# Experts begin on five full tiles of the first three batches, and the fourth batch is routed between their steps

## What is computed

```
# third layer, after the softmax and the weighting of the values
out = einsum('bnf,fd->bnd', out, Wout)
mu, var = mean(out), var(out)                       # over the 256 channels
out = (out - mu) * rsqrt(var + 1e-6) * ln_scale + ln_bias
x = x + tanh(g_xattn[1]) * out
# fourth layer, on X = layernorm(x)
logits = X @ Wg + bg                                # 8 experts
topv, topi = top_k(logits, 2); w = softmax(topv)
xs = X * w                                          # one row per token and choice
for e in range(8):                                  # H = 1024
    h = silu(xs @ W1[e]) * (xs @ W3[e]);  y = h @ W2[e]
    out = out + where(topi == e, y, 0).sum(choices)
x = x + tanh(g_ffn[1]) * (X + out)
```

## Time and profile before

| | us |
|---|---|
| median of 3 runs | 2034.28 (2030.84 to 2037.16) |
| the profiled execution | 2036.09 |
| its span, first to last instruction | 2034.4 |
| TensorE busy in the span | 1792.8 (88%) |
| VectorE busy | 1181.5 (58%) |
| ScalarE busy | 1116.2 (55%) |
| GpSimd busy | 423.8 (21%) |
| mean granted TensorE clock | 0.947 |

### The profile page before, as it was taken

How to read it: one execution, slowest core, us unless ns; L and a number is a source line. 1 busy time by engine, 2 the same in 40 slices (tenths; PEclk the granted TensorE clock), 3 DMA queues, 4 the chain that set the end, 5 groups by cost and what they waited for, 6 DMA issues and landing times. The chain is left out here.

```text
span 2034.4 us, 28113 instructions
## 1 busy us (share of the span) xinstructions
PE 1792.8 (88%) x9516; PEld 1121.3 (55%) x9516; DVE 1181.5 (58%) x2893; ACT 1116.2 (55%) x2334; POOL 423.8 (21%) x430
## 2 busy tenths in 40 slices
PE   5899998998996599999999999999982599999994
PEld 3455554554543234444444444445442599999994
DVE  4868768767772455545564465435644455555554
ACT  2566666666674155544554455445550467777662
POOL 3101200200201100000000002000202377766762
PEclk9999999999998699999999999899986799999997
DMA  3000000000000770000000001000001766666644
GB/s 94 1 21 1 21 1 1 22 1 1 1 1 0 263 245 1 21 1 0 1 21 1 0 1 43 1 0 1 23 1 51 249 212 202 203 208 214 217 152 140
DMA packets 122862, 134.13 MB, mean 66 GB/s; under 512 B 9248, under 2 KB 116640, under 8 KB 122720
## 3 DMA queue, kind: packets, MB, share of 16 engines
q1 hardware_dynamic: 115696, 119.45, 18.6%
q0 software_dynamic: 3744, 10.49, 1.4%
q10 hardware_dynamic: 3280, 2.40, 0.4%
HBM read 101.63 MB, written 30.69 MB: 65 GB/s over the span
## 5 line engine op out<-in xcount | busy, mean ns | idle before, releaser
L622 DVE TENSOR_REDUCE l_tile_max<-psum 128x1 f32<-128x512 f32 x512 | 341.8, 688 | 108.1 <-PE psum L345 106.7
L483 ACT ACTIVATE l_probs<-psum 128x1024 f32<-128x1024 f32 x256 | 248.3, 1022 | 99.3 <-PE psum L357 95.7
L345 PE MATMUL psum<-l_kT,l_qT 128*128 128x512 f32 x512 | 236.2, 469 | 40.9 <-DVE l_tile_max L622 37.6
L2013 POOL TENSOR_TENSOR moe_w_lo<-moe_w,moe_w_hi 128x512 fp32r<-128x512 f32 x179 | 233.2, 1303 | 139.6 <-ACT moe_w_hi L1886 138.9
L1380 DVE TENSOR_REDUCE l_row_max<-psum 128x2 f32<-128x1024 f32 x128 | 156.4, 1222 | 182.1 <-PE psum L1000 181.3
L1210 ACT ACTIVATE l_null_p<-l_s_null,l_neg_max 128x1 f32<-128x1 f32 x256 | 73.9, 289 | 285.2 <-DVE l_neg_max L1382 285.2
L1846 PE MATMUL psum<-moe_xs_hi,moe_w_hi 128*128 128x256 f32 x736 | 211.3, 287 | 1.4 <-DVE moe_xs_lo L1923 1.4
L1846 PE MATMUL psum<-moe_xs_lo,moe_w_hi 128*128 128x256 f32 x736 | 209.3, 284 | 0.0
L1846 PE MATMUL psum<-moe_xs_hi,moe_w_lo 128*128 128x256 f32 x736 | 209.3, 284 | 0.0
L1986 DVE TENSOR_TENSOR psum<-psum,moe_gate 128x256 f32<-128x256 f32 x184 | 79.3, 431 | 166.1 <-ACT moe_gate L1900 166.1
L1212 ACT ACTIVATE l_probs<-psum,l_neg_max 128x512 f32<-128x512 f32 x256 | 171.5, 670 | 0.0
(11 more groups left out here) (238 smaller groups left out, 3246.8 us busy)
## 6 DMA issues: line engine op xcount, KB each, us to landing
moe_w<-in_moe_w SPq DMA_DIRECT2D x276, 256.0 KB, 4.4
moe_sorted_x<-l_zeros SPq DMA_DIRECT2D x1, 17680.0 KB, 57.1
moe_xs<-moe_sorted_x SPq DMA_DIRECT2D x23, 272.0 KB, 2.9
l_ctxT<-in_ctxT SPq DMA_DIRECT2D x4, 1024.0 KB, 5.4
x_resid<-in_x SPq DMA_DIRECT2D x4, 512.0 KB, 10.1
l_raw<-in_ctx SPq DMA_DIRECT2D x4, 512.0 KB, 3.5
l_v_raw<-in_ctx SPq DMA_DIRECT2D x4, 512.0 KB, 3.6
l_wk<-in_wkv SPq DMA_DIRECT2D x1, 2048.0 KB, 16.1
```

The source lines that it names most:

```text
L345: nc.tensor.matmul(bank(max_bank(m)), qT[:, q % SLOTS, h, t * P:(t + 1) * P], kT[:, q % SLOTS, h // 2, half * BANK:(half + 1) * BANK], sta ...
L483: nc.scalar.activation(probs[:, n % PT_RING], wide(2 * (n % 2)), ACT.Exp, scale=SCALE).then_inc(exp_done, 1)
L622: nc.vector.reduce_max(tile_max[:, q % 2, t, h, half:half + 1], bank(max_bank(m)), AX_X).then_inc(max_read, 1)
L2013: nc.gpsimd.tensor_tensor(w13_lo[:, k % SPLITS], w13[:, slot_k, :, cols], w13_hi[:, k % SPLITS].bitcast(F32), ALU.subtract).then_inc(w13_s ...
```

## The change

- The router's buffers and steps move into a class `Router` that both layers use; what they compute is the same. In `layer1`, batch 2's routing is moved to earlier steps of `extra` (its norm now in groups 28 and 29, ranking in step (6, 0) in place of (6, 3), slots in (6, 2) in place of (7, 2)), and so are its PE and ACT parts. 
- The new number `FIRST` is 5: 3 batches of 512 tokens with 2 choices are 3072 rows, and with 8 experts at least 5 tiles of 256 rows are full whatever the routing. In the last group's idle DVE steps, `count_tiles`, `sum_tiles`, `note_used`, `list_experts` and `list_starts` list these five tiles.
- All of batch 3 that came after its projection leaves `layer1`. The block now ends with the projection.
- In `experts`, SP waits only for the scatter of three batches, loads tile 0's rows first, and then weights. For tile 5 it waits for the second list (`tiles_ready`), and loads that tile's rows after its weights, behind a wait for all scatters.
- Batch 3's work is cut into pieces that `route_last(k)` puts behind step k of each engine: PE at k = 10 (8 transposes), 12 (16 matmuls for the logits) and 17 (2 for the counts); ACT at 10, 17 (exponential) and 21 to 24 (scaling rows); DVE at 0 to 8, 10, 12, 14 to 18, 20, 22 to 26, 28, 29, 32 and 33; POOL at 22 to 29 (one scatter each).
- POOL splits w1 and w3 for the first five steps too. The `up` sums move to PSUM banks 4 to 6, both halves of a tile's result into one bank, and the copy out of it is one instruction.

```diff
+        self.FIRST = -(-(TOP * (self.T - self.TT) * P - self.E * (ROWS - 1)) // ROWS)
...
         else:
-            at = (first - 1, 1, 0), (first - 1, 1, 1), (first - 1, 2, 0), (first, 1, 0)
+            at = (first - 2, 2, 1), (first - 2, 3, 0), (first - 2, 3, 1), (first - 1, 1, 0)
...
-                keep_result(GROUPS - 1)
-                act.wait_ge(last_psum, 1)
-                nc.scalar.activation(rT[:, 0, :], bank(4), ACT.Copy).then_inc(last_act, 1)
-                weigh_second(s.B - 1)
-                for k in range(TOP):
-                    scale_rows(s.B - 1, k, range(T))
...
-                last_b = s.B - 1
-                dve.wait_ge(out_psum, T)
-                for _ in output_statistics(lambda t: bank(t)[:, 0:D]):
...
-                add_counts(last_b, bank(O_BANK))
-                choose_slots(last_b)
-                weigh_tops(last_b)
-                add_residual(last_b, range(T))
...
+        CHAIN = {"rT": 10, "logits": 12, "counts": 17, "exp": 17, "scale": 21, "scatter": 22}
...
-                sp.wait_ge(tiles_ready, 1)
+                sp.wait_ge(scattered, 16 * TOP * TB * LAST_B)
+                load_rows(0)
                 for m in range(PIECES):
-                    if m == W_SLOTS:
-                        sp.wait_ge(scattered, 16 * TOP * T)
-                        load_rows(0)
-                        load_rows(1)
                     i, part = divmod(m * PIECE, FT)
                     if part == 0:
+                        if i == FIRST:
+                            sp.wait_ge(tiles_ready, 1)
                         e = sp.value_load(expert_ids[0:1, i:i + 1], min_val=0, max_val=E - 1)
-                        if m >= W_SLOTS:
+                        if i >= 2 and i != FIRST:
                             load_rows(i)
                     load_weights(m)
+                    if m == 1:
+                        load_rows(1)
+                    if i == FIRST and part == FT - PIECE:
+                        sp.wait_ge(scattered, 16 * TOP * T)
+                        load_rows(FIRST)
...
+                round_weights(0)
+                round_rows(0)
+                for k in range(1, AHEAD):
+                    round_weights(k)
...
+                    if k == CHAIN["exp"]:
+                        act.wait_ge(tops, 1)
+                        nc.scalar.activation(router.top[:, 3, :], router.top[:, 2, :], ACT.Exp).then_inc(exped, 1)
...
+                dve.wait_ge(g["out_psum"], TB)
+                for _ in norm_out.statistics_steps(dve, lambda t: bank(t)[:, 0:D], LN_OUT_EPS):
+                    pass
+                split_down(0)
+                split_rows(0)
```

More of the change, by code:

```diff
@@ L1875, in _ @@
                         transposes(i + 1)
+                    route_last(k)
             @block.scalar
@@ L1936, in evacuate_y @@
                         dve.wait_ge(y_stored[i % 2], 16 * HALVES * (i // 2))
[L1937 to L1942 removed]
+                    nc.vector.tensor_copy(y_sb[:, i % 2].rearrange("p h d -> p (h d)"), y_bank(i)).then_inc(y_ready, 1)
@@ new lines, in add_output, with add_residual @@
+                def add_output(some):
+                    for t in some:
+                        last = nc.vector.scalar_tensor_tensor(out=last_tokens[:, t, :], in0=rows[:, t, :],
+                                                              scalar=norm_out.work[:, 1, t:t + 1], in1=last_tokens[:, t, :],
+                                                              op0=ALU.mult, op1=ALU.add)
+                    return last
+                def add_residual(some):
+                    for t in some:
+                        nc.vector.scalar_tensor_tensor(out=last_tokens[:, t, :], in0=routed[:, t, :], scalar=g["gates"][:, 3:4],
+                                                       in1=last_tokens[:, t, :], op0=ALU.mult, op1=ALU.add)
@@ L1982, in _ @@
+                last.then_inc(out_read, 1)
+                for k in range(1, AHEAD):
+                    split_down(k)
                 for k in range(STEPS + 1):
```

614 lines of the change are left out of this document (409 added, 205 removed).

## The result

The change makes the kernel faster, but by half of what was forecast. The median of four runs is 2014.91 us (2012.49 to 2021.83) beside 2035.72 (2030.84 to 2043.08) of the kernel before on the same chip: ratio 0.990, 95% interval 0.986 to 0.994. A second timing in a later comparison gave 2008.84 (2005.02 to 2015.28), ratio 0.988 (0.984 to 0.991). Both are well above the forecast of 1990.4 and its range to 2002. The profiled execution took 2012.49 us, 23.6 less than that of before, where 43.9 were expected.

The account below looks back on a forecast made before the run. PE was taken as full in the expert steps, with a 63 us hole ahead of them. A 50.3 us gain less 3.1, 0.8, 0.5 and 2.0 gave 43.9, so a median of 1990.4 us, range 1984 to 2002.

Parts of the forecast that it names:

- gain at `down(0)`: Expert layer's start: `down(0)` comes at 1554.8 instead of 1605.12, a gain of 50.3 us.
- router's PE work: Batch 3's logits matmuls, transposes and counts now stand in PE's full queue, adding 3.1 us.
- two table loads: ACT at step 17: two loads of 1.28 and an exponential, 2.8 us, mostly covered, leaving 0.8.
- DVE's pieces: Pieces in 24 expert steps, covered by 1.07 us idle per step and 0.9 margin; cost 0.5 us.
- POOL's lag: Extra scatters and stores make POOL lag 5.8 us after step 29, within 6.1 of margin; cost 0.
- tile 5's rows: PE waits near step 36 for rows fetched after the second list: 2.0 us, bounds 0 and 4.4.
- attention: Batch 2's work moved to earlier groups of the attention layer costs 0, bounds -3.6 and +2 us.
- third rival: No cover on DVE: each piece delays the hidden values by its whole length, +20 us, 2010; chance 0.05.
- signs that the prediction gave of being wrong: First `up` after 1550, repeated PE waits in steps 2 to 30, clock near 0.5 past step 3, projection ending after 1537.
- second rival: Last attention groups get longer: moved ranking makes PE wait for ACT's copies and DVE, two 3.57 waits, 1997.5; chance 0.06.
- fourth rival (clock): Waits between the first expert steps hold PE at 1.2 GHz, 4.32 us per step: slower, 2059; chance 0.02.
- The first (POOL behind): GpSimd falls behind: each scatter costs POOL its 1.27 twice, PE waits ten us for rows, 2000; chance 0.12.

Follow-up runs that it names:

- e8: Changed kernel with ScalarE copying instead of taking the exponential in step 17, so both table loads fall away: 2008.50 us, ratio 0.987.
- e3: Changed kernel with GpSimd's w1/w3 split cut to one column of each block for k = 8 to 38: 2001.52 us, ratio 0.984.
- e5: Changed kernel with the third batch's attention routing back in its old groups and the first list made behind the last group: 2009.85 us, ratio 0.987.
- e6: Changed kernel with VectorE and GpSimd taking turns in steps 0 to 29, old attention placement, residual adds in steps 42 to 47: 2000.62 us, ratio 0.983.
- e9: Changed kernel with turns in steps 0 to 29, residual adds in steps 42 to 47, tile 5's rows fetched two pieces earlier: 2001.62 us, ratio 0.984.
- e12: e9 with the list of remaining tiles made four steps earlier, ahead of VectorE's scaling of the rows: 1996.97 us, ratio 0.981.
- e13: e12 with row scatters issued ahead of GpSimd's split and tile 5's rows transposed in step 37 instead of 36: 2004.57 us, ratio 0.986.

## Why the prediction was wrong

How the layer starts was forecast rightly: the first weights, not the fourth batch, start it, and PE's first `up` came some ten us behind the end of the attention layer instead of 63. What the fourth batch's work costs between the steps was not. By the prediction's own steps, from the profiled executions:

| term | forecast | measured |
|---|---|---|
| gain at `down(0)` | 50.3 | 47.1 (1605.12 to 1558.02), 45.6 at the fourth SiLU |
| router's PE work | 3.1 | 2.7 in steps 11 and 13; the counts are inside step 18 |
| two table loads | 0.8 | step 20 comes no earlier when they are left out (e8) |
| DVE's pieces | 0.5 | 15.3 in steps 7 to 9 and 21 to 33; 14.4 by e3, up to the 37th SiLU |
| POOL's lag | 0 | 0, PE never waited for `w13_split` past the start |
| tile 5's rows | 2.0 | 1.3 in steps 36 and 37; 4.6 in e3, where the steps ahead are faster |
| attention | 0 | 4.1, of which 2.2 show (DVE starts at 1537.53, not 1535.3) |

The measured losses are the SiLUs' times beside the kernel before. From the fourth SiLU's gain they add up: 45.6, less 2.7, 2.8 (steps 17 to 20: counts, table loads and holds together), 15.3 and 1.3, is 23.5, and the profiled execution gained 23.6.

**The step that failed** is "DVE gets pieces in 24 steps. Its cover is 1.07 idle per step". The idle time was read rightly, but it isn't free time. In the earlier trace rows DVE's idle time is 1795.16 to 1796.23, and POOL's split starts 0.44 into it, at 1795.60, and lasts past its end. A piece put there runs in 0.2 if it reads PSUM or sums, and waits to the end of the split if not. (The term has a slip too, 1.3 less 0.9 is 0.4, which changes nothing.) The third rival said that a piece may cost its whole length; the truth was worse for small pieces and better for others: 0.18 became 1.92. Its chance of 0.05 was set by the idle time alone, and its time, 2010, was near the result for another reason than the one it gave. The wait of one small instruction then went through the hidden values to `down`, and where PE stood for 3.35 us its granted clock was 0.53 for 3 more. Of the signs that the prediction gave of being wrong, one came true plainly: PE waited again and again between steps 2 and 30. The projection's end, at 1537.1, is just past the 1537 of another.

The start was 3.2 late, and most of that is the same holding. The third piece of weights reached ACT at 1550.70, and the first gate began at 1552.95; the prediction's own steps give 1550.4 and 1552.6. The 2.9 behind that come from DVE: its first pieces, two residual adds that take 0.43 each when alone, stand beside two splits of POOL (1554.24 to 1556.98), and `down(0)` waits behind them. (The profile names no releaser for this wait; DVE's low part of the hidden values ends at 1557.93.)

```profile
1554.54 2.72 DVE L2116 SCALAR_TENSOR_TENSOR x_resid<-moe_rows,moe_out_work,x_resid 128x256 f32<-128x256 f32 x2
1558.02 0.55 PE L1993 MATMUL psum<-moe_w_hi,moe_hid_hi 128*128 128x256 f32 x1 [4.20 <-issue]
```

Behind this wait PE's clock is granted at 0.50 (1558 to 1560) and 0.69 (to 1562), which takes the gain down to 45.6 at the fourth SiLU.

**A second term failed**: the attention's, which was put at 0. From ACT's router instruction at 1393.16 (L1436; 1395.13 and L1262 in the kernel before) to PE's last matmul of the attention layer it takes 139.3 before, and 143.2 to 144.9 in all fifteen profiles with the change's placement. So it isn't scatter; in the profiled execution that row came 2.0 earlier by chance, and that hid half of the 4.1. PE waits 2.48 at 1482.30 for ACT's copy (L1414), with a clock of 0.54 from 1485 to 1490. That is the kind of wait that the second rival named, PE behind ACT's copies, at about half its price. e5 and e6, with the old placement, take 141.3, both of them. They follow the kernel before to within 0.02 for 94 us and are 3.2 late at 106 us. In between, behind a wait of PE for ACT's copy (3.09 in e5 as in the kernel before), their granted clock reads 0.51 and 0.50 for ten us, beside 0.87 before. Why it stays low there is open.

The table loads' row was right in that no pause stood behind them: the loads are at 1600.48 and 1602.10, 1.28 each, with the exponential at 1601.88 between them. The Trainium skill, ScalarE: Activation LUTs, section "What ACT_TABLE_LOAD costs", would have each switch at 2.66 with a drain. This trace doesn't agree: the exponential starts 1.42 behind the end of the ACT instruction ahead of it (1600.46), and the next gate, at 1603.40, 1.32 behind the exponential's end.

The fourth rival (clock) appeared only in pieces of a few us. The first (POOL behind) didn't show in the changed kernel. In e6, e9, e12 and e13 POOL did fall behind, and it was DVE that paid for it.

## What to carry to other kernels

Before work is put into an engine's idle time, look at what the other engines do in that time, not only at how long it is: in these runs a VectorE instruction that adds, copies or scales from SBUF to SBUF waits for the end of GpSimd's subtraction of two SBUF tiles, and of the next ones where they follow at once. Long GpSimd instructions beside many short VectorE ones are the bad case; remedies are to let them take turns (here 12.9 us for one wait and a new order on VectorE, which alone gave 3.3 at most), to give GpSimd the shorter of two operations (11.1 us, with the same order), or to keep an operand in PSUM. When a hold is cured, measure again and read the rows at the new loss: it can be a transfer that now comes late (e3), or the same hold in another place (e6, e9, e12, e13). And a term that is hidden by scatter in one profile shows when a stretch is measured between two fixed rows in all of them, as the attention's 4.1 does.

## What was not expected of the hardware

An instruction of 4 columns (L109, 0.17 alone) is held as long as a large one, 1.09. Splits in a row hold one VectorE instruction through all of them: 4.35 us beside three, 5.10 beside four. A split that is queued right behind a scatter holds VectorE from about 0.2 us ahead of its recorded start. And 3.4 us of waiting cost PE 5.1, because the granted clock behind it was 0.53, near the level of 1.2 GHz.
